# One block of a shared expert's tokens moved behind the routed experts in a one-core RWKV and mixture-of-experts layer

## The chip, the cores and the metric

The kernel runs on one core of a Trainium2 chip. The metric is the device time of one execution in microseconds (us). The median of three runs of the kernel before is 1152.21 us (1152.03 to 1153.88).

## What is computed

The input is x, 2048 tokens of 512 numbers in float32. Two parts follow each other. The first (time mixing and channel mixing) gives a new x. The second is a mixture of experts on h, the normalised x:

```python
x = x + attn(layernorm(x), ...)
h = layernorm(x)
scores = sigmoid(h @ gate_w)                      # 32 experts
sfc = scores + e_bias                             # chooses 2 of 4 groups, then 4 experts
combine = share of each chosen expert, 2.5 * score / sum of the 4 scores
routed = sum over the 4 experts of combine * relu(h @ Wu[e])**2 @ Wd[e]     # 512 -> 256 -> 512
shared = relu(h @ Wsu)**2 @ Wsd                                             # 512 -> 1024 -> 512
out = x + routed + shared
```

## The kernel before, in words

The program is written out engine by engine with semaphores. Nothing is scheduled by a planner: the order on each engine is the order of the code. Products in float32 precision are made of three matmuls of "hi" and "lo" halves (`split_product`, L595). A block is 512 tokens (`BLK`), a tile 128 (`P`). The shared expert's inner width of 1024 is cut into `NSI` = 8 slices of 128.

**Stages 1 and 2** compute the first part and are not touched.

**Stage 3** is the shared expert, in `NB` = 4 blocks of tokens (`pe_block3`, L1083). For each slice i, TensorE does `up(i)` (12 matmuls of 512 columns into bank 4 or 5) and then `down(i - 2)` (12 matmuls into banks 0 to 3, which sum over all slices). Between them ScalarE takes the bank through relu, squares it and makes the hi half (`act_inner`, L835), and GpSimd makes the lo half `ksp_lo` (`pool_inner`, L894). At a block's end ScalarE copies the four banks to `so` and SyncE's queue stores them to `shx_d`, the table in HBM on which half of the routed results are added later. The block's tokens come from HBM into the two slots of `hTb` (`sp_hTb`, L1216).

Beside stage 3, VectorE works out the routing (`routing_vector`, L1290): which tokens go to which expert, and from that a list of tiles, each of up to 128 tokens of one expert. It needs TensorE three times: `pe_counts` (L1108) and two calls of `pe_ids` (L1115). These stand in the blocks 1, 2 and 3, each behind slice 2 (`BETWEEN_AT`). When `rows_i` is there, GpSimd can begin to gather tokens (`first_gathers`, L1663), which it does behind its last `ksp_lo` of stage 3.

**Stage 4** is the routed experts: 84 tiles here. For each, GpSimd gathers 128 rows by an indirect DMA, TensorE transposes them (L1497), multiplies with `Wu` of the expert (L1505), transposes the result (L1513) and multiplies with `Wd` (L600). ScalarE scales the result into a ring of four buffers `yo` (`take_y`, L1575), and GpSimd adds it to rows in HBM by an indirect DMA with addition (`add_rows`, L1674): even tiles to `res_d` (which holds x), odd tiles to `shx_d`. Additions to one table must wait for each other. Weights of eight experts lie in a ring `w8`, loaded by SyncE's queue (`load`, L1222).

**Stage 5** waits until all additions have landed, loads `res_d` and `shx_d` in 8 parts each (`stage5_sync`), adds them on VectorE (`stage5_vector`) and stores the sums to `out` from ScalarE's queue (`stage5_scalar`).

```python
            pe_block3(pe, 0, router=True)
            pe_block3(pe, 1, between=pe_counts)
            pe_block3(pe, 2, between=lambda pe: pe_ids(pe, (0, 1)))
            pe_block3(pe, 3, between=lambda pe: pe_ids(pe, (2, 3)))
```

Of the kernel before, what the change touches and what calls it, by code (L numbers as in the profile page):

```python
# [24 lines left out]
P = 128  # L25
T, H = 2048, 512
NT = T // P
BT = 4
# [45 lines left out]
def program(nc, a, out, scratch):  # L74
# [13 lines left out]
    with ctx:  # L88
# [9 lines left out]
        shx_rows = shx_d[0:T].rearrange("(b j p) d -> b p j d", j=BT, p=P)  # L98
        spare_rows = [m[T:T + 2 * P].rearrange("(n p) (u d) -> p n u d", p=P, u=2) for m in (res_d, shx_d)]
# [69 lines left out]
        wsu = [at(f"wsu_{s}", [P, C, SI], R, 16 * n) for n, s in enumerate(("hi", "lo"))]  # L169
        wsd = [at(f"wsd_{s}", [P, NSI, H], R, 32 + 16 * n) for n, s in enumerate(("hi", "lo"))]  # L170
# [14 lines left out]
        ebias = at("ebias", [P, E], F, 182.0625)  # L185
# [15 lines left out]
        xg = [at(f"xg{n}", [P, H + E], F, 2.125 * (n % 6) + (186 if n < 6 else 64)) for n in range(XRING)]  # L201
# [8 lines left out]
        last = [at(f"last{n}", [P, 8, NT // 8 * H], F, kb) for n, kb in enumerate((104, 64))]  # L210
# [624 lines left out]
        def act_inner(act, n, i, router=None):  # L835
# [3 lines left out]
            nc.scalar.activation(ra[:, i % 2], bank[4 + i % 2][:], ACT.Relu).then_inc(sem("kc_free"), 1)  # L839
# [65 lines left out]
        def pe_inner_up(pe, n, i, weights, rhs):  # L905

            pe.wait_ge(sem("kc_free"), n + 1)
            split_product(bank[4 + i % 2][:], lambda s, c: weights[s][:, c, i * P:(i + 1) * P],
                          rhs, C).then_inc(sem("kc_in"), 1)

        def pe_inner_down(pe, n, i, last, rhs):

            pe.wait_ge(sem("klo_in"), n + 3)
            for j in range(BT):
                for k, (l, r) in enumerate(((0, 0), (0, 1), (1, 0))):
                    m = nc.tensor.matmul(bank[j][:], ksp[l][:, i % 2, j * P:(j + 1) * P], rhs(r),  # L916
                                         start=i == 0 and k == 0, stop=i == last and k == 2)
            m.then_inc(sem("vc_done"), 1)
# [162 lines left out]
        BETWEEN_AT = 2  # L1081

        def pe_block3(pe, b, router=False, between=None):  # L1083
# [17 lines left out]
            for i in range(NSI):  # L1101
                pe_inner(pe, NB - 1, i, N3 + b * NSI + i, up, down, router, NB * BT)
                if i == BETWEEN_AT and between:
                    between(pe)
# [65 lines left out]
        def stage3_scalar(act):  # L1170
            act_hi3(act, *ORDER3[:4])
            act_block3(act, 0, router=True)
            with act.Fori(1, NB) as b:
# [27 lines left out]
        def stage3_gpsimd(pool):  # L1201
            pool_block3(pool, 0, first=True)
            with pool.Fori(1, NB - 1) as b:
                pool_block3(pool, b)
            pool_block3(pool, NB - 1, last=True)
# [47 lines left out]
        def stage3_sync(sp):  # L1253

            sp.wait_ge(sem("trT_in"), NB * C)
# [12 lines left out]
            sp.wait_ge(sem("sc_in"), NB)  # L1268
            sp.dma_start(ebias[:], a["L0_ffn_e_bias"].partition_broadcast(P)).then_inc(sem("eb_in"), 16)
            for b in range(NB):  # L1270
                if b + 2 < NB:
                    sp.wait_ge(sem("kc_in"), N3 + (b + 1) * NSI)
                    sp.wait_ge(sem("hb_in"), 16 * (b + 2))
                    if b + 2 == NB - 1:
                        sp.wait_ge(sem("ht_st"), 16 * C * NB + 16)
                    sp_hTb(sp, b + 2)
                if b == 1:
                    first_experts(sp)
                if b == 1:
                    sp.wait_ge(sem("share_in"), 1)  # L1280
                    sp.wait_ge(sem("h_st"), 16 * NB + 16)
                    sp.dma_start(share_rows, share[:]).then_inc(sem("share_st"), 16)
                if b == 2:
# [536 lines left out]
```

## Time and profile before

| what | value |
|---|---|
| median of three runs | 1152.21 us |
| the profiled execution | 1152.85 us |
| its span | 1151.0 us |
| mean granted TensorE clock | 0.972 of 2.4 GHz |
| TensorE busy | 1058.1 us (92%) |
| VectorE, ScalarE, GpSimd busy | 574.8, 539.7, 436.0 us |
| DMA | 192.91 MB, mean 168 GB/s |

The span is the stretch from the first to the last instruction or transfer of the profiled execution; 1.85 us of its own time lie outside it. Shares are averages over stages with different limits, so each stage has to be read by itself.

### The profile page before, as it was taken

Reading aid. Unit: us, or ns where it says so; the run is one execution under the profiler, and the core shown is the slowest. Engines: PE = TensorE matmul, PEld = TensorE weight load, DVE = VectorE, ACT = ScalarE, POOL = GpSimd, SP = SyncE. Lnnn points to the kernel's source line nnn. Section 1 sums busy time; section 2 is a strip of 40 time slices with the busy share of each in tenths; the row PEclk is TensorE's granted clock in tenths of the full one; section 3 lists DMA queues with packets and bytes.
Section 4 is the critical chain, followed back from the end, with each engine's and each line's share of the span. In section 5 each row is a group of like instructions: output and inputs, shape, how many; then the busy total and the mean of one; then the engine's idle time right before and its main releaser. Section 6 shows DMA issues by size and latency. Waiting matters only on the chain.

```text
span 1151.0 us, 17191 instructions
## 1 busy us (share of the span) xinstructions
PE 1058.1 (92%) x4892; PEld 849.6 (74%) x4893; DVE 574.8 (50%) x1126; ACT 539.7 (47%) x896; POOL 436.0 (38%) x327
## 2 busy tenths in 40 slices
PE   1999989999999999999989999998999999999940
PEld 0446768888788878878867888886888888888830
DVE  6976764925570475320072886322545544455532
ACT  3643536333333333243353334335777766677730
POOL 1012212321222132112252234226767777888730
PEclk9898999999999999999998999998999999999985
DMA  8605176526421642342472228016898999988679
GB/s 285 228 1 183 55 249 249 179 74 219 147 92 60 233 158 97 121 150 95 131 289 110 110 111 265 37 37 162 168 282 182 247 233 270 327 140 136 84 137 373
DMA packets 96914, 192.91 MB, mean 168 GB/s; under 512 B 12888, under 2 KB 32344, under 8 KB 96352
## 3 DMA queue, kind: packets, MB, share of 16 engines
q1 hardware_dynamic: 76464, 147.43, 36.8%
q0 software_dynamic: 18816, 39.87, 18.5%
q10 hardware_dynamic: 1584, 4.98, 1.2%
q8 instruction: 27, 0.44, 0.1%
q14 instruction: 23, 0.19, 0.1%
HBM read 137.78 MB, written 60.03 MB: 172 GB/s over the span
## 4 chain that ended last, share of the span: by engine, by line
PE 82%; DMA 7%; DVE 7%; issue 2%; ACT 2%; SPq 1%; POOL 0%; ACTq 0%; POOLq 0%; DVEq 0%
PE bank L600 36%; PE bank L916 22%; PE bank L1505 11%; PE bank L517 4%; PE bank L1497 3%; DMA shx_d<-yo,idy 2%; DMA last<-shx_d 2%; PE bank L1513 1%; DMA res_d<-yo,idy 1%; PE bank L924 1%; SPq L1751 1%; PE bank L934 1%; DMA f<-in_L_attn_x 1%; DMA z_d<-zo 1%; PE bank L978 1%
## 5 line engine op out<-in xcount | busy, mean ns | idle before, releaser
L897 POOL TENSOR_TENSOR ksp_lo<-ra,ksp_hi 128x512 fp32r<-128x512 f32 x96 | 146.3, 1524 | 470.1 <-ACT ksp_hi L846 470.1
L1632 DVE TENSOR_TENSOR wds<-w,wds 128x1024 fp32r<-128x1024 f32 x84 | 103.1, 1227 | 186.4 <-ACT wds L1573 186.4
L1505 PE MATMUL bank<-w,xT 128*128 x672 | 160.3, 382 | 0.4 <-SPq L71 0.3
L916 PE MATMUL bank<-vring,ksp_hi 128*128 128x512 f32 x512 | 159.5, 393 | 0.0
L1505 PEld LDWEIGHTS bank<-w,xT 128*128 128x128 f32 x672 | 128.1, 191 | 21.1 <-issue 1.4
L839 ACT ACTIVATE ra<-bank 128x512 f32<-128x512 f32 x96 | 57.3, 597 | 173.9 <-PE bank L600 170.4
L600 PE MATMUL bank<-wds,aT 128*128 128x512 f32 x504 | 137.6, 408 | 1.4 <-DVE aT L1627 1.3
L846 ACT ACTIVATE ksp_hi<-ra 128x512 fp32r<-128x512 f32 x96 | 60.7, 632 | 124.9 <-PE bank L916 124.4
L916 PEld LDWEIGHTS bank<-vring,ksp_hi 128*128 128x128 f32 x512 | 95.6, 188 | 20.0
L600 PE MATMUL bank<-xcT_hi,wck_lo 128*128 128x512 f32 x256 | 101.8, 398 | 0.0
L600 PEld LDWEIGHTS bank<-wds,aT 128*128 128x128 f32 x504 | 88.5, 189 | 18.0 <-DVE aT L1627 1.8
L600 PE MATMUL bank<-xcT_lo,wck_hi 128*128 128x512 f32 x256 | 101.6, 397 | 0.0
L600 PE MATMUL bank<-xcT_hi,wck_hi 128*128 128x512 f32 x256 | 101.3, 396 | 0.0
L916 PE MATMUL bank<-vring,ksp_lo 128*128 128x512 f32 x256 | 99.9, 390 | 0.0
L1580 ACT ACTIVATE yo<-bank,xg 128x512 f32<-128x512 f32 x84 | 57.8, 688 | 85.7 <-PE bank L600 54.2
L1659 POOL DMA_INDIRECT xg<-h_d,idc x60 | 84.7, 1412 | 18.3 <-issue 16.2
L1573 ACT ACTIVATE wds<-w 128x1024 fp32r x84 | 88.1, 1049 | 0.1
L600 PE MATMUL bank<-hTb,wsu_hi 128*128 128x512 f32 x256 | 79.8, 393 | 0.0
L361 POOL TENSOR_TENSOR mix_lo<-mx,mix_hi 128x512 fp32r<-128x512 f32 x16 | 22.4, 1416 | 121.5 <-ACT mix_hi L419 121.5
L1681 POOL DMA_INDIRECT res_d<-yo,idy x36 | 58.0, 1612 | 26.3 <-DMA res_d<-yo,idy 13.5
L1681 POOL DMA_INDIRECT shx_d<-yo,idy x36 | 57.4, 1594 | 20.0 <-DMA shx_d<-yo,idy 9.3
L841 ACT ACTIVATE ra<-ra 128x512 f32<-128x512 f32 x96 | 60.7, 632 | 3.1
(260 smaller groups left out, 1916.4 us busy)
## 6 DMA issues: line engine op xcount, KB each, us to landing
vring<-wcv_d SPq DMA_DIRECT2D x64, 512.0 KB, 3.3
w<-in_L_ffn_Wu SPq DMA_DIRECT2D x32, 512.0 KB
w<-in_L_ffn_Wd SPq DMA_DIRECT2D x32, 512.0 KB
hT_d<-hT SPq DMA_DIRECT2D x16, 512.0 KB, 3.3
hTb<-hT_d SPq DMA_DIRECT2D x4, 2048.0 KB, 9.4
raw_wcv<-in_L_attn_Wcv SPq DMA_DIRECT2D x4, 1024.0 KB, 6.6
raw_wck<-in_L_attn_Wck SPq DMA_DIRECT2D x4, 1024.0 KB, 9.6
f<-in_L_attn_x SPq DMA_DIRECT2D x4, 1024.0 KB, 6.9
```

Of the source, the lines that this page charges most:

```text
L600: i = nc.tensor.matmul(dst, lhs(l, c), rhs(r, c), start=c == 0 and k == 0, stop=c == n - 1 and k == 2)
L839: nc.scalar.activation(ra[:, i % 2], bank[4 + i % 2][:], ACT.Relu).then_inc(sem("kc_free"), 1)
L841: nc.scalar.activation(ra[:, i % 2], ra[:, i % 2], ACT.Square).then_inc(sem("sq"), 1)
L846: nc.scalar.activation(ksp[0][:, i % 2], ra[:, i % 2], ACT.Copy).then_inc(sem("khi_in"), 1)
L897: nc.gpsimd.tensor_tensor(ksp[1][:, i % 2], ra[:, i % 2], ksp[0][:, i % 2], ALU.subtract).then_inc(sem("klo_in"), 1)
L916: m = nc.tensor.matmul(bank[j][:], ksp[l][:, i % 2, j * P:(j + 1) * P], rhs(r), start=i == 0 and k == 0, stop=i == last and k == 2)
L1505: m = nc.tensor.matmul(bank[2 + u][:, 0:EI], xT4[:, u, c * P:(c + 1) * P], slot_of(wu8[:, :, c * EI:(c + 1) * EI], e), start=c == 0, stop= ...
L1573: nc.scalar.activation(wds[:, u, 0], slot_of(wd8, e), ACT.Copy).then_inc(sem("wh4"), 1)
L1580: nc.scalar.activation(yo[:, t % YRING], bank[6 + u][:], ACT.Copy, scale=xg[t % XRING][:, bass.ds(H + e, 1)]).then_inc(sem("y4"), 1)
L1632: nc.vector.tensor_tensor(wds[:, u, 1], slot_of(wd8, e), wds[:, u, 0], ALU.subtract).then_inc(sem("wl4"), 1)
L1659: pool.indirect_dma_start(out=xg[t % XRING][:], out_offset=None, in_=h_d, in_offset=bass.IndirectOffsetOnAxis(ap=row.bitcast(U32), axis=0) ...
L1681: pool.indirect_dma_start(out=(res_d, shx_d)[u], out_offset=bass.IndirectOffsetOnAxis(ap=row.bitcast(U32), axis=0), in_=yo[:, k % YRING], ...
```

## The change

One block of the shared expert, tokens 1536 to 2047, leaves stage 3 and is computed behind the last routed tile. TensorE does `up3(0)` and `up3(1)` between its last three steps of stage 4, then the other slices (banks 0 and 1 for up, 2 to 5 for down). ScalarE and GpSimd do their part of it behind their last `take_y` and `add_rows`. `hT3`, the block's tokens, is loaded into two slots of the weight ring when expert 25 is done. The rows of `shx_d` of this block no longer hold the shared expert's result: they are set to zero by eight stores before, and in stage 5 VectorE adds the block's sums straight out of the four banks. Stage 5 now has six parts of 256 rows for the other 1536 tokens and a part `rest` for these 512. It loads all of `res_d` as soon as that table's additions have landed, then `shx_d`, and all stores go out from SyncE's queue.

The routing's TensorE work stands earlier: `pe_counts` behind slice 1 of block 1, `pe_ids` behind slices 1 and 4 of block 2. The bias `ebias` is loaded at the start of stage 3 instead of behind the scores. The buffers of stage 4 (`xT4`, `a4`, `aT4`, `yo`, `wds`, half of `xg`) lie elsewhere, because the weights of the shared expert must stay in place. Weight loads of experts 0 to 6 are issued in block 1 and not in blocks 1 and 2.

```diff
+        hT3 = at("hT3", [P, 2, C, BLK], R, 96)
...
-        xT4 = at("xT4", [P, 2, C * P], F, 0)
-        a4 = at("a4", [P, 2, EI], F, 8)
-        aT4 = at("aT4", [P, 2, 2, EI], R, 10)
-        yo = at("yo", [P, YRING, H], F, 14)
-        wds = at("wds", [P, 2, 2, EI // P * H], R, 34)
+        xT4 = at("xT4", [P, 2, C * P], F, 160.5)
+        a4 = at("a4", [P, 2, EI], F, 92.75)
+        aT4 = at("aT4", [P, 2, 2, EI], R, 180.5)
+        yo = at("yo", [P, YRING, H], F, 172.5)
+        wds = at("wds", [P, 2, 2, EI // P * H], R, 64)
...
-        last = [at(f"last{n}", [P, 8, NT // 8 * H], F, kb) for n, kb in enumerate((104, 64))]
+        PARTS = 6
+        last = [at(f"last{n}", [P, PARTS, 2 * H], F, kb) for n, kb in enumerate((112, 136))]
+        rest = [at(f"rest{n}", [P, BT, H], F, kb) for n, kb in enumerate((64, 72))]
...
-            pe_block3(pe, 1, between=pe_counts)
-            pe_block3(pe, 2, between=lambda pe: pe_ids(pe, (0, 1)))
-            pe_block3(pe, 3, between=lambda pe: pe_ids(pe, (2, 3)))
+            pe_block3(pe, 1, between={1: pe_counts})
+            pe_block3(pe, 2, between={1: lambda pe: pe_ids(pe, (0, 1)), 4: lambda pe: pe_ids(pe, (2, 3))})
...
+            for n in range(BT):
+                for u in range(2):
+                    sp.dma_start(open_rows[:, n, u], zrow[:].bitcast(F)).then_inc(sem("spare_st"), 16)
...
             dve.wait_ge(sem("eb_in"), 16)
-            dve.wait_ge(sem("num_in"), 2)
+            dve.wait_ge(sem("sc_in"), NB)
+            dve.wait_ge(sem("ht_st"), 16 * C * NB + 16)
...
+        def up3(pe, i):
+            pe_inner_up(pe, N4 + i, i, wsu, lambda s, c: hT3[:, s, c], kc=0)
+
+        def down3(pe, i):
+            pe_inner_down(pe, N4 + i, i, NSI - 1, lambda s: wsd[s][:, i], to=2)
...
             final = GROUP * passes + GROUP - 1
+            pe.wait_ge(sem("hb_in"), 16 * NB)
             turn(final, 1)
+            up3(pe, 0)
             down(final - 1, 0)
+            up3(pe, 1)
             down(final, 1)
+            for i in range(2, NSI):
+                up3(pe, i)
+                down3(pe, i - 2)
+            down3(pe, NSI - 2)
+            down3(pe, NSI - 1)
...
+            end = sp.value_load(ends_i[0:1, E - WSLOTS + 1:E - WSLOTS + 2], min_val=1, max_val=SLOT_TILES)
+            wait_apart(sp, sem("d4"), end + 2)
+            sp.dma_start(hT3[:].bitcast(F), hT_d[NB - 1]).then_inc(sem("hb_in"), 16)
...
-            for u in range(2):
+            for u, rows in enumerate((res_d, shx_d)):
                 wait_apart(sp, sem(f"y_st{u}"), 8 * GROUP * passes + 8 * GROUP)
+                for n in range(PARTS):
+                    sp.dma_start(last[u][:, n], part_rows(rows)[:, n]).then_inc(sem(f"part_in{n}"), 16)
+                sp.dma_start(rest[u][:], rest_rows(rows)).then_inc(sem(f"part_in{PARTS}"), 16)
             for n in range(PARTS):
-                for to, rows in zip(last, (res_d, shx_d)):
-                    sp.dma_start(to[:, n], part_rows(rows[0:T])[:, n]).then_inc(sem(f"part_in{n}"), 16)
+                sp.wait_ge(sem("o5"), n + 1)
+                sp.dma_start(part_rows(out[0])[:, n], last[0][:, n]).then_inc(sem("o_st"), 16)
+            for j in range(BT):
+                sp.wait_ge(sem("o5"), PARTS + 1 + j + 1)
+                sp.dma_start(rest_rows(out[0])[:, j], rest[0][:, j]).then_inc(sem("o_st"), 16)
+            sp.wait_ge(sem("o_st"), 16 * (PARTS + BT))
...
+            dve.wait_ge(sem(f"part_in{PARTS}"), 16 + 32)
+            nc.vector.tensor_tensor(rest[0][:], rest[0][:], rest[1][:], ALU.add).then_inc(sem("o5"), 1)
+            dve.wait_ge(sem("o5"), PARTS + 1)
+            for j in range(BT):
+                dve.wait_ge(sem("sum3"), j + 1)
+                nc.vector.tensor_tensor(rest[0][:, j], rest[0][:, j], bank[2 + j][:], ALU.add).then_inc(sem("o5"), 1)
...
         def stage5_scalar(act):
-            for n in range(PARTS):
-                act.wait_ge(sem("o5"), n + 1)
-                act.dma_start(part_rows(out[0])[:, n], last[0][:, n]).then_inc(sem("o_st"), 16)
-            act.wait_ge(sem("o_st"), 16 * PARTS)
+            for i in range(NSI):
+                act_inner(act, N4 + i, i, kc=0)
+
+        def stage5_gpsimd(pool):
+            for i in range(NSI):
+                pool_inner(pool, N4 + i, i)
```

Two places show how the order of instructions moves. The first is TensorE at the end of stage 4. `ident,a` is the transpose of a tile's inner values, `wds,aT` the product with `Wd` of six matmuls a tile. Before, these are its last instructions (x12 are the last two tiles):

```order
L1513 MATMUL bank<-ident,a_195 128x128 x2
L600 MATMUL bank<-wds,aT_196 128x512 x6
L1513 MATMUL bank<-ident,a_195 128x128 x2
L600 MATMUL bank<-wds,aT_196 128x512 x12
L88 UNCONDITIONAL_BRANCH
```

In the change, from the same transpose on (`hT_149` is the tile `hT3`):

```order
L1522 MATMUL bank<-ident,a_196 128x128 x2
L604 MATMUL bank<-wds,aT_197 128x512 x6
L1522 MATMUL bank<-ident,a_196 128x128 x2
L604 MATMUL bank<-hT_149,wsu_hi 128x512 x2
L604 MATMUL bank<-hT_149,wsu_lo 128x512
L604 MATMUL bank<-hT_149,wsu_hi 128x512 x2
L604 MATMUL bank<-hT_149,wsu_lo 128x512
L604 MATMUL bank<-hT_149,wsu_hi 128x512 x2
L604 MATMUL bank<-hT_149,wsu_lo 128x512
L604 MATMUL bank<-hT_149,wsu_hi 128x512 x2
L604 MATMUL bank<-hT_149,wsu_lo 128x512
L604 MATMUL bank<-wds,aT_197 128x512 x6
```

Twelve matmuls of `up3(0)` now stand ahead of the product of the last tile but one, and another twelve (`up3(1)`) ahead of that of the last tile; the remaining 168 follow.

The second place is SyncE's queue at the end of the program. Before, from the last weight load on, it holds the reads of `passes_i` and 16 loads in turns; two pairs of the eight are shown:

```order
L1226 DMA w_181<-in_L_ffn_Wd 128x2x512
L1730 REGISTER_ALU
L1730 COMPARE_AND_BRANCH
L1460 TENSOR_LOAD passes_i
L1460 ISA x2
L70 ISA
L1751 DMA last_201<-res_d 128x1024
L1751 DMA last_202<-shx_d 128x1024
L1751 DMA last_201<-res_d 128x1024
L1751 DMA last_202<-shx_d 128x1024
L1751 DMA last_201<-res_d 128x1024
L1751 DMA last_202<-shx_d 128x1024
```

In the change:

```order
L1759 DMA hT_149<-hT_d 128x4096
L1463 TENSOR_LOAD passes_i
L1463 ISA x2
L70 ISA
L1771 DMA last_202<-res_d 128x1024 x6
L1772 DMA rest_204<-res_d 128x4x512
L1771 DMA last_203<-shx_d 128x1024 x6
L1772 DMA rest_205<-shx_d 128x4x512
L1775 DMA out<-last_202 128x1024 x6
L1778 DMA out<-rest_204 128x512 x4
L88 UNCONDITIONAL_BRANCH
```

The load of `hT3` is new, the two tables are no longer loaded in turns, and the stores of the result have moved to this queue.

## Rows read from the trace of the kernel before

**Rows 1.** The page: the chain that ended last, by engine; costly groups.

```profile
PE 82%; DMA 7%; DVE 7%; issue 2%; ACT 2%; SPq 1%; POOL 0%; ACTq 0%; POOLq 0%; DVEq 0%
...
L1505 PE MATMUL bank<-w,xT 128*128 x672 | 160.3, 382 | 0.4 <-SPq L71 0.3
...
L839 ACT ACTIVATE ra<-bank 128x512 f32<-128x512 f32 x96 | 57.3, 597 | 173.9 <-PE bank L600 170.4
L600 PE MATMUL bank<-wds,aT 128*128 128x512 f32 x504 | 137.6, 408 | 1.4 <-DVE aT L1627 1.3
```

**Rows 2.** Chain of waits, 700 to 800 us: start, length (us), what.

```profile
700.12 1.38 PE bank L1121 x32
...
734.25 8.16 PE bank L600 x36
...
745.13 1.38 PE bank L1121 x32
...
749.34 2.72 PE bank L916 x12
...
771.10 8.17 PE bank L916 x36
...
784.05 1.94 PE bank L1497 x8
...
786.07 3.31 PE bank L1505 x8
```

**Rows 3.** Timeline of GpSimd, 700 to 790 us: start, length, instruction, [idle before].

```profile
774.62 1.29 POOL L897 TENSOR_TENSOR ksp_lo<-ra,ksp_hi 128x512 fp32r<-128x512 f32 x1 [4.15 <-ACT ksp_hi L846]
776.09 1.22 POOL L1659 DMA_INDIRECT xg<-h_d,rows_i  x1 [0.18 <-issue]
```

**Rows 4.** Timeline of TensorE, 1095 us to the end.

```profile
1104.60 0.44 PE L1513 MATMUL bank<-ident,a 128*128 128x128 f32 x2 [0.59 <-DVE a L1623]
1104.93 1.64 PE L600 MATMUL bank<-wds,aT 128*128 128x512 f32 x6
1107.92 1.66 PE L600 MATMUL bank<-wds,aT 128*128 128x512 f32 x6 [1.34 <-DVE aT L1627]
```

**Rows 5.** Timeline of ScalarE, then of GpSimd, 1084 to 1112 us.

```profile
1109.73 0.69 ACT L1580 ACTIVATE yo<-bank,xg 128x512 f32<-128x512 f32 x1 [2.24 <-DMA shx_d<-yo,idy]
...
1111.40 1.54 POOL L1681 DMA_INDIRECT shx_d<-yo,idy  x1 [1.48 <-DMA shx_d<-yo,idy]
```

**Rows 6.** Chain of waits, the last 51 us.

```profile
1100.67 1.73 PE bank L1505 x8
...
1111.40 4.51 DMA shx_d<-yo,idy
...
1115.98 0.35 SPq L1751
...
1124.77 21.91 DMA last<-shx_d
...
1146.70 1.23 DVE last L1756
```

**Rows 7.** Busy time by stretch: PE, PEld, DVE, ACT, POOL, then PEclk, DMA share, GB/s.

```profile
784.00:788.00 4.00, 3.87 (x13) 3.15 (x14) 0.05 (x1) 2.14 (x3) 3.09 (x4) 0.50 1.03 368
1108.00:1112.00 4.00, 1.58 (x6) 0.97 (x6) 0.00 (x0) 0.69 (x1) 2.14 (x2) 1.00 0.83 100
1121.00:1126.00 5.00, 0.00 (x0) 0.00 (x0) 2.45 (x2) 0.00 (x0) 0.00 (x0) 0.50 1.02 370
1136.00:1146.00 10.00, 0.00 (x0) 0.00 (x0) 3.22 (x3) 0.00 (x0) 0.00 (x0) 0.50 1.02 419
```

**Rows 8.** Timeline of VectorE, 612 us to the end.

```profile
673.14 2.29 DVE L1405 TENSOR_TENSOR hot_p<-iota_p,small 128x2048 f16<-128x2048 f32 x1
...
700.93 2.29 DVE L1405 TENSOR_TENSOR hot_p<-iota_p,small 128x2048 f16<-128x2048 f32 x1 [13.21 <-PE bank L1121]
...
712.90 1.76 DVE L1410 TENSOR_TENSOR hot_q<-hot_f,token 128x1536 f16<-128x1536 f16 x1
...
728.32 0.15 DVE L1434 TENSOR_SCALAR passes_i<-passes_i 128x1 int32<-128x1 int32 x1
...
1121.01 1.22 DVE L1756 TENSOR_TENSOR last<-last,last 128x1024 f32<-128x1024 f32 x1 [13.15 <-DMA last<-shx_d]
```

**Rows 9.** Timeline of GpSimd, 600 to 701 us: one slow `ksp_lo`.

```profile
673.64 2.94 POOL L897 TENSOR_TENSOR ksp_lo<-ra,ksp_hi 128x512 fp32r<-128x512 f32 x1 [4.14 <-ACT ksp_hi L846]
```

More of the change, by code:

```diff
@@ L98, in program @@
         shx_rows = shx_d[0:T].rearrange("(b j p) d -> b p j d", j=BT, p=P)
+        open_rows = shx_d[T - BLK:T].rearrange("(n p) (u d) -> p n u d", p=P, u=2)
         spare_rows = [m[T:T + 2 * P].rearrange("(n p) (u d) -> p n u d", p=P, u=2) for m in (res_d, shx_d)]
@@ L184, in program @@
         top8 = at("top8", [P, NT, 8], F, 181.5625)
-        ebias = at("ebias", [P, E], F, 182.0625)
+        ebias = at("ebias", [P, E], F, 200)
         small = at("small", [P, 8, NT * GROUPS], F, 182.1875)
@@ L903, in stage2_gpsimd, with pe_inner_up, pe_inner_down @@
                     pool_inner(pool, b * NCI + i, i)
-        def pe_inner_up(pe, n, i, weights, rhs):
+        def pe_inner_up(pe, n, i, weights, rhs, kc=4):
             pe.wait_ge(sem("kc_free"), n + 1)
-            split_product(bank[4 + i % 2][:], lambda s, c: weights[s][:, c, i * P:(i + 1) * P],
+            split_product(bank[kc + i % 2][:], lambda s, c: weights[s][:, c, i * P:(i + 1) * P],
                           rhs, C).then_inc(sem("kc_in"), 1)
-        def pe_inner_down(pe, n, i, last, rhs):
+        def pe_inner_down(pe, n, i, last, rhs, to=0):
             pe.wait_ge(sem("klo_in"), n + 3)
@@ L915, in pe_inner_down @@
                 for k, (l, r) in enumerate(((0, 0), (0, 1), (1, 0))):
-                    m = nc.tensor.matmul(bank[j][:], ksp[l][:, i % 2, j * P:(j + 1) * P], rhs(r),
+                    m = nc.tensor.matmul(bank[to + j][:], ksp[l][:, i % 2, j * P:(j + 1) * P], rhs(r),
                                          start=i == 0 and k == 0, stop=i == last and k == 2)
-            m.then_inc(sem("vc_done"), 1)
+                if to and i == last:
+                    m.then_inc(sem("sum3"), 1)
+            if not (to and i == last):
+                m.then_inc(sem("vc_done"), 1)
         def pe_logits(pe, b, c):
@@ L1102, in pe_block3 @@
                 pe_inner(pe, NB - 1, i, N3 + b * NSI + i, up, down, router, NB * BT)
-                if i == BETWEEN_AT and between:
-                    between(pe)
+                if i in between:
+                    between[i](pe)
             down(NSI - 2)
@@ L1172, in stage3_scalar @@
             act_block3(act, 0, router=True)
-            with act.Fori(1, NB) as b:
+            with act.Fori(1, NB - 1) as b:
                 act_block3(act, b)
@@ L1202, in stage3_gpsimd @@
             pool_block3(pool, 0, first=True)
-            with pool.Fori(1, NB - 1) as b:
-                pool_block3(pool, b)
-            pool_block3(pool, NB - 1, last=True)
+            pool_block3(pool, 1)
+            pool_block3(pool, NB - 2, last=True)
         def sp_raw3(sp, k):
@@ L1253, in stage3_sync @@
         def stage3_sync(sp):
+            sp.dma_start(ebias[:], a["L0_ffn_e_bias"].partition_broadcast(P)).then_inc(sem("eb_in"), 16)
             sp.wait_ge(sem("trT_in"), NB * C)
@@ L1267, in stage3_sync @@
             sp_hT(sp, NB - 1)
[L1268 to L1276, printed above, removed]
+            for n in range(BT):
+                for u in range(2):
+                    sp.dma_start(open_rows[:, n, u], zrow[:].bitcast(F)).then_inc(sem("spare_st"), 16)
+            for b in range(NB - 1):
+                if b == 0:
+                    sp.wait_ge(sem("kc_in"), N3 + NSI)
+                    sp.wait_ge(sem("hb_in"), 16 * 2)
+                    sp_hTb(sp, 2)
                 if b == 1:
                     first_experts(sp)
-                if b == 1:
                     sp.wait_ge(sem("share_in"), 1)
@@ L1604, in stage4_scalar @@
             a_hi(0, 0)
+            act.wait_ge(sem("bs_st"), 16 * NB)
             for t in range(2, YRING + 2):
@@ L1777, in _ @@
             stage4_gpsimd(pool)
+            stage5_gpsimd(pool)
         @block.scalar
```

27 lines of the change are left out of this document (13 added, 14 removed).

## The prediction

> **What bounds the kernel now.** I read the page's chain first, then the chain in order of time around the block that moves, the timelines of the engines where stage 3 ends and where stage 4 ends, and busy time by stretch. TensorE is 82% of the chain, and in stage 4 its two large groups of matmuls waited 0.4 and 1.4 us in all [rows 1]. So whatever leaves TensorE's queue before the last tile comes off the time in full. The block that moves is one unbroken run of TensorE work, from 734.25 to 779.27 us, 45.0 us, of which `pe_ids` has 1.4 to 1.5 [rows 2]. The reader should then look at the other end. TensorE starts its last product at 1107.92 [rows 4], and from there the program is one chain: ScalarE's last scaling at 1109.73 and GpSimd's last addition at 1111.40 [rows 5], its landing at 1115.91, the loads of both tables until 1146.68, one VectorE addition until 1147.93, and the store, with which the span ends at 1151.0 [rows 6]. In those 41.4 us TensorE has nothing to do. The change puts 43.5 us of it there, so the question is by how much the new TensorE work sticks out behind the transfers.
>
> **What leaves stage 3.** 192 matmuls, at 2.72 us for 12 [rows 2]: 43.5 us. The `pe_ids` of block 3 goes to block 2 and keeps its 1.4. What follows stage 3 hangs on its last block and moves with it: the first gather was issued 0.18 us after the last `ksp_lo` [rows 3], and TensorE stood still from 779.27 to 784.05 before its first transposes [rows 2]. I keep this gap as it was. Its cover is the routing: in block 2 everything must be known 43.5 us sooner. VectorE stood still 13.21 us because `pe_ids` had its place behind slice 2 of block 2 [rows 8]. Behind slice 1 it starts one up and one down earlier, 5.44 us, and VectorE's next masks with it: the fourth pair, done at 714.66, would be done near 709.2. TensorE reaches its new place for it, behind slice 4, at about 712.5 (slice 3 begins at 701.5, when the first `pe_ids` is done [rows 2]; four runs of 2.72, the 1.4 of `pe_ids` in them before and after alike). That leaves some 3 us. The list of owners (728.47) comes at 723.0 and the list of rows about 1.5 us later, ahead of the last `ksp_lo` of block 2, now near 731. Nothing waits, so the routing's part of the change is worth nothing by itself. Of `ebias` the same holds.
>
> **The other edits of stage 3.** The eight zero stores of 128 KB and the earlier weight loads stand on SyncE's queue behind the stores of `hT` and in block 1, where the next load of tokens is wanted tens of us later; cost nothing. If that cover were gone, TensorE would start block 2 late. The load of `hT3` (2 MB) goes out when expert 25 is done and is wanted only behind the last tile. It competes with gathers and additions, as 1 MB of weights for each expert did all through stage 4, where TensorE lost under 2 us in all [rows 1]; nothing, at most 2 us. The moved buffers have the same sizes and readers; nothing.
>
> **What is added behind stage 4**, in the times of the trace of before, so that the 43.5 us are taken off at the end. The turn of the last tile starts at 1104.60 and what follows it at 1104.93 [rows 4].
> - `up3(0)` 2.72, product of the last tile but one 1.36 (half of 12), `up3(1)` 2.72: the last product starts at 1111.73, 3.8 us later than before.
> - ScalarE began its scaling 1.81 us after that product's start [rows 4, 5]: 1113.54 to 1114.23.
> - Only then comes its first relu, 0.60 [rows 1], which frees a bank. `up3(2)` starts at 1114.95 and ends at 1117.67. TensorE has stood still from 1113.1, 1.8 us.
> - `down3(0)` wants `ksp_lo`, on GpSimd behind the last addition. That was issued 0.98 us after the scaling and took 1.54 [rows 5]: 1115.21 to 1116.75. `ksp_lo` takes 1.29 [rows 3], to 1118.04. 0.4 us of waiting.
> - Eight downs and five ups, 13 times 2.72: 35.4 us, to 1153.5.
> - VectorE's last addition out of a bank has half the columns of the 1.23 us one [rows 6]; I take 0.7, with 0.25 to wake. Then the store until the end of the span, 3.07 [rows 6]: 1157.5.
>
> **Sum.** 1157.5 less 43.5 is a span of 1114.0, against 1151.0: 37.0 us less. The profiled execution's own time was 1152.85, which gives 1115.8; it lies 0.64 above the median, so from the median I forecast **1115.2 us**.
>
> **The cover of the loads.** Loads and stores must be done before TensorE, or they are the bound. Before, from the first issue (1115.98) to the last landing (1146.68) [rows 6], 16 loads and some 7 stores of 0.524 MB moved, 12.1 MB in 30.7 us. Now `res_d` can start when its last addition has landed: the product starts at 1107.65, and with the 1.81, 0.69, 0.98 and 4.5 us above [rows 5, 6] that is 1115.6. The other table's addition lands near 1120, hidden behind 4.2 MB of loads. So 8.4 MB of loads and 6 stores, 11.5 MB, at the same pace take 29.3 us, to 1145.3. VectorE's addition of the 2048 columns of `rest` is twice 1.23, to 1147.8. TensorE's first bank is ready nine matmuls before its end, at 1151.4. There are 3.6 us to spare. At the 370 GB/s of the first stretch of loads [rows 7] it would be 1.9 us more, at 419 it would be sooner. The page *DMA: Bandwidth & Descriptors* of the Trainium skill (section Bandwidth, "Where 436 GB/s comes from") puts what HBM gives a core at about 358 GB/s; by that, an estimate, the 11.5 MB take 32.2 us, with 2.2 us until the stream runs (the first MB was there after 5.0 us [rows 6, 8]) `rest` would be added only at 1152.6, and the sum would be about 1 us more. The trace speaks against it, since 10 us of mixed loads and stores ran at 419 GB/s.
>
> **The rivals.**
> - *The DMAs are the bound.* Place: `rest`, last of 14 loads, behind six stores. For it: the share of the DMA engines is 1.02 in both stretches [rows 7], so nothing hides there, and the last addition to `shx_d` now has to land beside 4 MB of loads. If the loads of `shx_d` start only at 1130, 4.2 MB and 3.1 MB of stores take 18.6 to 19.8 us, and the additions of `rest` and of four banks end near 1155: about 1116. With a slower pace yet, up to 1121. Against: 3.6 us to spare. Chance 0.14.
> - *GpSimd's last `ksp_lo` waits for VectorE.* One `ksp_lo` took 2.94 us where 1.29 is usual, while VectorE was in the 2.29 us mask that began half a microsecond before it [rows 3, 8, 9]. The page *GPSIMD Engine Reference* of the Trainium skill (section Key points) says the two share their SBUF interfaces, when VectorE has two SBUF inputs; the trace agrees. The last `ksp_lo` falls near 1148.8, just where `rest` (2.45 us, two inputs) may be added. TensorE wants it 0.65 us after its usual end, so the loss is up to 1.8 us: 1115.2 to 1117.0. The other seven have some 6 us to spare. Chance 0.16.
> - *The routing is late.* If VectorE gains nothing by the earlier `pe_ids` (its fourth pair at 714.66 as now), TensorE waits 2.2 us at slice 4: 1117.4. More if the gathers wait too. Chance 0.06.
> - *Slower: TensorE runs the tail at its lower clock.* Place: the stops of 0.6, 1.8 and 0.4 us at the seam. After the stop of 4.8 us the granted clock was 0.50 (1.2 GHz), and 8 matmuls took 3.31 us [rows 2, 7] where stage 4's usual step has the same for 1.73 [rows 6]; so the price is 0.91 us for each us of matmuls. Over all 46 us of the tail that is 42 us, and the time 1157. It decides from 41 us of the tail at the lower clock on. Against: after the stop of 1.34 us the last six took 1.66, like the six before (1.64) [rows 4], and the clock was 1.00 in that stretch [rows 7]. A single spell like that at 784 would cost 2 to 4 us. Chance 0.03 for slower.
> - *The work is not taken off the front*, or stage 4 pays for it: something in block 2 or among the first tiles waits for what block 3 used to cover (the eighth expert's weights, gathers beside a busy VectorE), by 7 us to 35 us: 1122 to 1150. I see nothing for it in the rows. Chance 0.05.
>
> **How the numbers follow.** The forecast as it stands has 0.56. Its own range is 1113.5 to 1117: below because the last store is now 256 KB instead of 512, above for `hT3`. To that the first three rivals are added, all below 1121; what is left out is the last two and a little on either side. Range 1113.0 to 1121.0. A measurement of this kernel can tell 0.2%, 2.3 us, from no change. All cases but the slower one and the far end of the last are faster by more: 0.96 faster, 0.01 within, 0.03 slower.
>
> **What would show it.** Right: stage 4's first transposes near 740.5; TensorE's block at the end unbroken for 13 runs of 2.72 us, with one stop of about 1.8 us before `up3(2)` and one under 1 us before `down3(0)`; its last matmul 3.5 to 4.5 us before the end of the span; VectorE adds `rest` before it waits for a bank; and the chain, read from its end, goes to TensorE and not to the loads. Wrong: an addition of `rest` that ends after TensorE (DMA bound), a `ksp_lo` above 2 us as the last one, a stop at L1126 (`pe_ids`) in block 2, a granted clock of 0.50 behind the seam, or first transposes later than 742.

## The result, and the profile after

The changed kernel took 1123.3 us (median of four runs), the kernel before 1152.12 us beside it: a ratio of 0.973, interval 0.970 to 0.977. The forecast was 1115.2 us with a range of 1113.0 to 1121.0. So the sign and most of the gain came as forecast, and some 8 us of it did not. One of the four runs, of 1206.88 us at a granted clock of 0.856 where the others had 0.984 to 0.989, is left out of the ratio, and the median of the other three is 1122.99 us. The profiled execution took 1123.62 us, 1.92 us more than its span.

The page: span, busy time of each engine, shares of its chain, and the second of the two groups of matmuls of [rows 1]:

```profile
span 1121.7 us, 17152 instructions
...
PE 1061.7 (95%) x4892; PEld 849.4 (76%) x4893; DVE 580.5 (52%) x1129; ACT 536.4 (48%) x892; POOL 434.3 (39%) x327
...
PE 74%; DMA 7%; DVE 7%; issue 6%; POOL 3%; ACT 2%; POOLq 0%; DVEq 0%; ACTq 0%; SPq 0%
...
L604 PE MATMUL bank<-wds,aT 128*128 128x512 f32 x504 | 138.2, 410 | 1.4 <-DVE aT L1645 1.3
```

The chain of the changed kernel where stage 3 ends, in order of time (start, length, what), which answers to [rows 2]:

```profile
728.51 8.17 PE bank L920 x36
...
737.89 3.56 issue
741.45 1.91 PE bank L1506 x8
```

Stage 3 now ends at 736.69 and the first transposes start at 741.45, after the same gap of 4.76 us. Forecast was 740.5. The front of the program is as forecast, but for 0.9 us.

The chain of the tail, which answers to [rows 6], and the timeline of VectorE in it (start, length, engine, line, operation, in brackets the idle time before and what ended it):

```profile
1069.96 8.22 PE bank L604 x36
...
1078.32 0.70 ACT yo L1597
...
1079.81 1.54 POOL shx_d L1699
1081.35 1.33 POOL ksp_lo L901
...
1082.72 3.02 PE bank L920 x12
...
1110.22 6.13 PE bank L920 x27
...
1116.45 2.66 DVE rest L1790 x4
```

```profile
1096.42 9.09 DVE L1784 TENSOR_TENSOR last<-last,last 128x1024 f32<-128x1024 f32 x6 [23.25 <-DMA last<-shx_d]
1105.49 2.29 DVE L1786 TENSOR_TENSOR rest<-rest,rest 128x2048 f32<-128x2048 f32 x1
1116.45 2.66 DVE L1790 TENSOR_TENSOR rest<-rest,bank 128x512 f32<-128x512 f32 x4 [8.67 <-PE bank L920]
```

The program now ends with TensorE, not with the loads: VectorE has added `rest` and stands still 8.67 us until TensorE's first bank is there. The last tile's turn is at 1069.55, and from it to the end of the span are 52.15 us. The forecast had 52.9 (1104.60 to 1157.5).

So the stretch in which the time went astray is the one that the change seemed to leave alone, stage 4:

| stretch | before | forecast | after | after less forecast |
|---|---|---|---|---|
| start to first transposes | 784.05 | 740.5 | 741.45 | +0.9 |
| first transposes to last tile's turn | 320.55 | 320.55 | 328.10 | +7.55 |
| last tile's turn to end of span | 46.40 | 52.9 | 52.15 | -0.7 |
| span | 1151.0 | 1114.0 | 1121.7 | +7.7 |

A tile of stage 4 takes TensorE 3.775 us where nothing is waited for. I took the starts of all 84 tiles' `Wu` products from the timeline; what the distance from one to the next has above 3.775 is called the tile's loss. Tiles are counted from 0. Before, five tiles between 928 and 1002 us lost 0.3 to 1.0 us each, 3.0 together. After, eight between 868 and 962 us lost 0.4 to 1.3 each, 5.0 together, and three others stand out: the third tile (tile 2, 749 us) with 1.67, and tiles 70 and 71 (1012 and 1020 us) with 3.81 and 0.77. These last two are the largest piece, 4.58 us. There the trace has, on SyncE's queue, GpSimd, ScalarE and TensorE:

```profile
1001.15 0.35 SPq L1759 DMA_DIRECT2D hT<-hT_d  x1
1001.91 1.58 POOL L1699 DMA_INDIRECT res_d<-yo,idy  x1 [0.31 <-issue]
...
1014.25 1.58 POOL L1699 DMA_INDIRECT res_d<-yo,idy  x1 [4.98 <-DMA res_d<-yo,idy]
...
1013.59 0.69 ACT L1597 ACTIVATE yo<-bank,xg 128x512 f32<-128x512 f32 x1 [5.68 <-DMA res_d<-yo,idy]
...
1013.94 0.60 PE L1506 MATMUL bank<-ident,xg 128*128 128x128 f32 x4
1017.14 0.44 PE L1522 MATMUL bank<-ident,a 128*128 128x128 f32 x2 [2.59 <-DVE a L1641]
1017.47 2.54 PE L604 MATMUL bank<-wds,aT 128*128 128x512 f32 x6
```

and in the chain, which runs through it:

```profile
1001.91 11.55 DMA res_d<-yo,idy
```

The load of `hT3` is issued at 1001.15, an addition to `res_d` right behind it at 1001.91, and that addition lands only after 11.55 us. Before, the last addition took 4.5 us [rows 6], and four in the middle of its stage 4, beside weight loads, took 7.3 to 9.1. ScalarE may not overwrite its `yo`, so it stands still 5.68 us and takes no bank, VectorE gets nothing, and TensorE stands still 2.59 us. Then its six matmuls take 2.54 us instead of the usual 1.38 to 1.40. The windows (us; PE, PEld, DVE, ACT, POOL busy, granted clock, share of the DMA engines, GB/s) show why:

```profile
1004.00:1008.00 4.00, 4.00 (x23) 3.43 (x22) 2.14 (x4) 2.91 (x6) 3.53 (x5) 1.00 1.04 398
1008.00:1012.00 4.00, 4.00 (x23) 3.44 (x22) 1.02 (x3) 0.00 (x0) 1.27 (x1) 1.00 0.96 262
1012.00:1016.00 4.00, 2.54 (x14) 2.00 (x12) 0.48 (x1) 2.42 (x5) 1.58 (x1) 1.00 0.36 98
1016.00:1020.00 4.00, 2.86 (x9) 2.20 (x10) 3.27 (x6) 2.81 (x6) 3.26 (x3) 0.75 0.83 132
1020.00:1024.00 4.00, 4.00 (x20) 3.37 (x19) 1.73 (x4) 2.89 (x5) 3.39 (x3) 0.83 0.95 150
```

First the DMA engines are full (1.04, 398 GB/s), then ScalarE does nothing for 4 us, then TensorE has a hole, and after the hole the granted clock is 0.75 and 0.83: part of these 8 us ran at 1.2 GHz and not at 2.4.

The kernel before has the first half of this pattern on a smaller scale. There the two weight loads of one expert, 0.5 MB each, stand right ahead of an addition (SyncE's queue, then the chain, then GpSimd):

```profile
917.10 0.38 SPq L1224 DMA_DIRECT2D w<-in_L_ffn_Wu  x1
917.58 0.46 SPq L1226 DMA_DIRECT2D w<-in_L_ffn_Wd  x1
...
917.64 9.12 DMA res_d<-yo,idy
...
927.57 1.58 POOL L1681 DMA_INDIRECT res_d<-yo,idy  x1 [2.55 <-DMA res_d<-yo,idy]
```

The addition lands after 9.12 us, and the tile at 928 us, the first of the five above, loses 0.77. In both traces the small losses lie during such series of weight loads or up to 11 us behind one. No run takes the weight loads away, so that these cause the small losses is not shown.

The tile at 749 us, and one in stage 3 where a half product waited for GpSimd:

```profile
752.81 1.62 PE L604 MATMUL bank<-wds,aT 128*128 128x512 f32 x6 [1.35 <-DVE aT L1645]
687.18 0.47 PE L920 MATMUL bank<-wsd_hi,ksp_hi 128*128 128x512 f32 x1 [0.28 <-POOL ksp_lo L901]
```

### The profile page after: what moved, and what is told of

It is laid out like the page before. It is cut to its first block, busy times and chain, and to the rows that moved or that the text cites. A ratio compares the mean times of both kernels' runs of the same rounds, so it can differ in the third digit from the quotient of the medians.

```text
span 1121.7 us, 17152 instructions
## 1 busy us (share of the span) xinstructions
PE 1061.7 (95%) x4892; PEld 849.4 (76%) x4893; DVE 580.5 (52%) x1129; ACT 536.4 (48%) x892; POOL 434.3 (39%) x327
## 4 chain that ended last, share of the span: by engine, by line
PE 74%; DMA 7%; DVE 7%; issue 6%; POOL 3%; ACT 2%; POOLq 0%; DVEq 0%; ACTq 0%; SPq 0%
PE bank L604 34%; PE bank L920 22%; PE bank L1514 7%; PE bank L521 5%; DMA res_d<-yo,idy 4%; DMA shx_d<-yo,idy 2%; PE bank L1506 2%; PE bank L931 1%; PE bank L1522 1%; POOL shx_d L1699 1%; POOL xg L1677 1%; PE bank L941 1%; DMA f<-in_L_attn_x 1%; PE bank L985 1%; DVE bns L311 1%
## 5 line engine op out<-in xcount | busy, mean ns | idle before, releaser
L1677 POOL DMA_INDIRECT xg<-h_d,idc x60 | 81.1, 1351 | 18.3 <-issue 16.5
L604 PE MATMUL bank<-hTb,wsu_hi 128*128 128x512 f32 x192 | 60.1, 394 | 1.1 <-DMA hTb<-hT_d 1.1
```

What stands on the lines that cost most here:

```text
L604: i = nc.tensor.matmul(dst, lhs(l, c), rhs(r, c), start=c == 0 and k == 0, stop=c == n - 1 and k == 2)
L1677: pool.indirect_dma_start(out=xg[t % XRING][:], out_offset=None, in_=h_d, in_offset=bass.IndirectOffsetOnAxis(ap=row.bitcast(U32), axis=0) ...
```

## The experiments

All are edits of the changed kernel. The theory: the load of `hT3`, one DMA of 2 MB with 16 KB for each partition, gets in the way of an addition, and that costs the 4.6 us. Rivals: the place itself (short tiles there), the wait for `bs_st` at 749 us, or nothing but scatter. The first four ran beside a kernel before of 1154.22 us.

**The changed kernel again**, no edit.

> The changed kernel once more, unedited, to see how much of the 7.7 us that it lies above the forecast is the same in every execution. In its first trace the routed tiles lost 8.6 us against a steady 3.775 us for each tile; 1.7 of that behind the first three tiles, 3.8 and 0.8 right behind the load of hT3, and the rest in steps of 0.3 to 1.3 us between 867 and 966 us. Theory A (two fixed costs of the change, the wait for the store of the shared expert and the load of hT3): the first and the hT3 losses come again at the same tiles within 0.5 us, the others wander; span 1118 to 1123. Theory B (chance of the DMAs only): the losses lie elsewhere, and the span is anywhere from 1114 to 1124.

Measured: 1118.57 us (1115.74 to 1123.6), ratio 0.9695 (0.965 to 0.974). The profiled execution, 1120.71 us, has the loss at the same two tiles, 3.11 and 1.04, with an addition that landed after 11.09 us. The stop at the third tile is not in it. So theory A holds for the load and fails for the third tile; and the kernel scatters by 8 us.

**The load left out.**

```diff
-            pe_inner_up(pe, N4 + i, i, wsu, lambda s, c: hT3[:, s, c], kc=0)
+            pe_inner_up(pe, N4 + i, i, wsu, lambda s, c: wsd[s][:, c], kc=0)
...
-            pe.wait_ge(sem("hb_in"), 16 * NB)
...
-            end = sp.value_load(ends_i[0:1, E - WSLOTS + 1:E - WSLOTS + 2], min_val=1, max_val=SLOT_TILES)
-            wait_apart(sp, sem("d4"), end + 2)
-            sp.dma_start(hT3[:].bitcast(F), hT_d[NB - 1]).then_inc(sem("hb_in"), 16)
```

> The load of hT3 (2 MB) and the wait for it are left out; the moved block then multiplies by wsd where it should by hT3, with the same shapes, so its result is another. Theory A: the load keeps additions waiting, one landing took 11.6 us, and cost 4.6 us at two tiles; time 4 to 5 us below the unedited kernel, and no tile period above 5 us after 1000 us. Theory B: the additions are at their limit anyway and the loss only moves; under 2 us below the unedited kernel.

Measured: 1115.49 us (1110.48 to 1118.42), ratio 0.9656 (0.961 to 0.970). The stretch in its windows, whole where the kernel with the load has its hole:

```profile
1008.00:1012.00 4.00, 4.00 (x23) 3.45 (x22) 1.90 (x3) 3.10 (x7) 3.08 (x4) 1.00 0.85 142
1012.00:1016.00 4.00, 4.00 (x23) 3.45 (x22) 1.90 (x3) 2.94 (x6) 3.39 (x3) 1.00 0.87 149
1016.00:1020.00 4.00, 4.00 (x23) 3.45 (x22) 1.90 (x3) 3.02 (x6) 3.39 (x3) 1.00 0.80 140
```

No tile after 966 us lost anything. The load is the cause of that loss, not the place. By the medians it is worth 3.1 us here (1118.57 less 1115.49), where 4 to 5 were expected, and the two ranges overlap.

**The wait for `bs_st` moved** to the first tile's `take_y`, the first writer of a `yo`.

```diff
+                elif t == 0:
+                    act.wait_ge(sem("bs_st"), 16 * NB)
...
-            act.wait_ge(sem("bs_st"), 16 * NB)
```

> ScalarE waits for the store of so to shx_d only right before it writes yo for the first tile, not ahead of the relu and copies of the tiles 1 to 4. Theory A: the store was issued at 738.9 and the wait ended at about 751.2, 2.5 us after ScalarE could have gone on; the first use of yo is at about 753, so the stop vanishes and TensorE's first product starts 1.3 to 1.7 us sooner; time 1.3 to 1.7 us less. Theory B: the store is not what ended that wait, or the time is lost again at the first additions, which are behind the same store; under 0.5 us.

Measured: 1118.84 us (1117.95 to 1123.76), ratio 0.971 (0.967 to 0.975), no different from the unedited kernel: theory B, or a stop that comes too seldom to show in a median. Tiles 70 and 71 lose 3.65 and 0.75.

**The same 2 MB in rows of 2 KB**, eight DMAs one behind the other.

```diff
-            sp.dma_start(hT3[:].bitcast(F), hT_d[NB - 1]).then_inc(sem("hb_in"), 16)
+            for s in range(2):
+                for c in range(C):
+                    sp.dma_start(hT3[:, s, c].bitcast(F), hT_d[NB - 1][:, s, c]).then_inc(sem("hb_in"), 16)
```

> The load of hT3 goes out at the same moment and with the same bytes, but as eight DMAs whose rows are 2 KB instead of one with rows of 16 KB. Theory A1 (the long rows keep the additions from their turn on each DMA engine): the loss behind 1001 us falls from 4.6 to under 2 us; time 3 to 4 us below the unedited kernel. Theory A2 (it is the bytes: 2 MB at once take 5 to 6 us of all engines whatever their rows): the loss stays 4 to 5 us.

Measured: 1116.36 us (1115.52 to 1117.6), ratio 0.9679 (0.965 to 0.971), 2.2 us below the unedited kernel. GpSimd's and TensorE's rows, which answer to those at 1014.25 and 1017.14 of the changed kernel, and a window:

```profile
1007.95 1.58 POOL L1699 DMA_INDIRECT res_d<-yo,idy  x1 [2.98 <-DMA res_d<-yo,idy]
1010.84 0.44 PE L1522 MATMUL bank<-ident,a 128*128 128x128 f32 x2 [0.60 <-DVE a L1641]
```

```profile
1012.00:1016.00 4.00, 4.00 (x23) 3.44 (x22) 2.22 (x4) 3.38 (x9) 3.39 (x3) 1.00 0.86 149
```

The same bytes from the same tile on: the addition lands after 9.55 us instead of 11.1 to 11.6, TensorE stops 0.60 us, the clock stays at 1.00, and the two tiles lose 0.98 us in place of 4.2 to 4.6. So 2 us less of landing took 3 us or more off the loss, since the last 2 us of delay also bring the lower clock. That is theory A1's outcome for the loss. But the edit changes two things. Each of the eight DMAs has its own issue on SyncE's queue, and the eight take 5.21 us (from 996.86) where the one of 2 MB took 0.35. Short rows and a load that goes out spread over 5 us can't be told apart by this run.

The next four ran beside a kernel before of 1153.19 us. **Two DMAs with rows of 8 KB:**

```diff
+            for s in range(2):
+                sp.dma_start(hT3[:, s].bitcast(F), hT_d[NB - 1][:, s]).then_inc(sem("hb_in"), 16)
```

> The load of hT3 at the same moment as two DMAs with rows of 8 KB, between the one with 16 KB (tiles 70 and 71 lost 3.8 and 0.8 us, or 3.1 and 1.0) and the eight with 2 KB (1.0 us in all). If the length of a row is what keeps an addition waiting, the loss lies between, 2 to 4 us, and the addition's landing between 9.6 and 11.6 us. If the number of DMAs matters and not the rows, it is nearer to 4.6 us.

Measured: 1118.96 us (1114.61 to 1125.88), ratio 0.9707 (0.967 to 0.975); landing 11.41 us, stop 2.45 us, loss 3.36 and 1.10. As 16 KB, and so the outcome that was expected if not the rows matter but the number of DMAs. The two are issued within 0.84 us. By this run the spread issue is at least as good an explanation of the eight DMAs' gain as their short rows; the rows of 16 KB sent as eight DMAs, over fewer partitions each, would tell more, and were not run.

**One piece a tile**, the eight pieces each behind a tile of their own:

```diff
+            for s in range(2):
+                for c in range(C):
+                    wait_apart(sp, sem("d4"), end + (2 + s * C + c))
+                    sp.dma_start(hT3[:, s, c].bitcast(F), hT_d[NB - 1][:, s, c]).then_inc(sem("hb_in"), 16)
```

> The same eight pieces with rows of 2 KB, but each waits for one tile more, so that 256 KB go out every 3.8 us instead of 2 MB at once. Theory A: what is left of the loss behind expert 25 (1.0 us) goes too, all tiles from 60 on take 3.775 us, and the time is 0 to 1 us under that of the small rows sent at once (1116.4 median). Rival: SyncE's waits cost something that I don't see, or pieces late in the stage meet the last additions; 1 us or more above it.

Measured: 1116.57 us (1115.73 to 1118.65), ratio 0.9674 (0.965 to 0.970). Nothing is lost after 966 us, as expected; the medians of this and of small rows alone are 0.2 us apart, less than they scatter.

**Small rows, and the seam closed:** ScalarE and GpSimd do slices 0 and 1 of the moved block ahead of the last two `take_y` and `add_rows`, not behind both.

```diff
+                    act_inner(act, N4 + k - n, k - n, kc=0)
                     take_y(passes, t - 2, t % 2, before)
...
+                    if last and k >= GROUP - 2:
+                        pool_inner(pool, N4 + k - GROUP + 2, k - GROUP + 2)
                     add_rows(i, k, idy[:, k:k + 1])
...
-            for i in range(NSI):
+            for i in range(2, NSI):
```

> The small rows at once, and in addition ScalarE takes the moved block's slices 0 and 1 through relu, square and hi half ahead of its last two scalings, and GpSimd their lo halves ahead of its last two additions. The stops of TensorE behind the last routed tile (1.4 us before up3(2), 0.2 and a slower first matmul before down3(0)) should vanish, the last additions come 0.3 to 1.5 us later, which nothing waits for, since rest was added 8.7 us before its first bank. Expected 1.4 to 1.7 us less than the small rows alone, 1114.8 in the median. Rival: the stops reappear elsewhere (TensorE's products of the last two tiles wait), 0 to 0.5 us less.

Measured: 1113.77 us (1112.68 to 1114.95), ratio 0.9652 (0.963 to 0.967). At the seam TensorE has no idle time behind the last turn any more (the last product of stage 4, then `up3(2)`, then `down3(0)`):

```profile
1069.17 1.52 PE L604 MATMUL bank<-wds,aT 128*128 128x512 f32 x6
1070.53 0.62 PE L604 MATMUL bank<-hT,wsu_hi 128*128 128x512 f32 x2
...
1073.25 0.39 PE L920 MATMUL bank<-wsd_hi,ksp_hi 128*128 128x512 f32 x1
```

From `up3(2)` to `down3(0)` are 2.72 us; in the changed kernel, with a slow start and the stop of 0.17, 1079.55 to 1082.72 are 3.17, and the stop of 1.37 stands ahead of it. The gain is more than the 1.4 to 1.7 us expected: 2.6 us in the medians (of two batches), and 2.2 in the traces from the last turn on.

**Pieces paced, and the seam closed**, the last two diffs together, the pieces one a tile:

> One piece of hT3 a tile, and the seam as in the run before: the two gains add, 1113.5 to 1115.5 us in the median, below both the kernel before and the changed one.

Measured: 1113.72 us (1112.21 to 1116.43), ratio 0.9659 (0.964 to 0.968). As expected. Either of the two beats both kernels, and they don't differ.

The last four were to put a number on the load, beside a kernel before of 1154.0 us. **A second load of `hT3`**, seven tiles behind the first:

```diff
             sp.dma_start(hT3[:].bitcast(F), hT_d[NB - 1]).then_inc(sem("hb_in"), 16)
+            sp.wait_ge(sem("hb_in"), 16 * NB)
+            wait_apart(sp, sem("d4"), end + 9)
+            sp.dma_start(hT3[:].bitcast(F), hT_d[NB - 1]).then_inc(sem("hb_in"), 16)
```

> The load of hT3 issued a second time, seven tiles after the first, with the same 2 MB and the same rows of 16 KB; the result is unchanged. If the load is what holds the addition back and stops TensorE: a second loss of 4 to 4.6 us appears some 27 us after the first (near 1040), with an addition to res_d or shx_d that lands after 11 us, and the time is 4 to 5 us above the unedited kernel of this batch. Rival, the loss at tiles 70 and 71 belongs to that place (short tiles of one expert, a low clock there) and not to the load: no second loss, and the time is that of the unedited kernel within 1 us.

**The unedited kernel, the kernel without the load, and the one with rows of 2 KB**, with the edits shown above:

> The changed kernel as it is, as the measure for the other three of this batch. Expected: a median between 1118 and 1122, with the loss of 4.2 to 4.6 us at tiles 70 and 71 in the trace.

> The load of hT3 and the wait for it left out again; the moved block's up products read the weights of wsd in its place, so that the shared expert's share of tokens 1536 to 2047 is something else. If the load's price is what its stretch of the trace shows, the median is 4 to 5 us below the unedited kernel of this batch, near 1115. Rival, the price is partly made good elsewhere or hidden by the scatter: 1 to 3 us.

> hT3 loaded by eight DMAs with rows of 2 KB at the same moment. By the traces so far it keeps 1.0 us of the loss: the median 3 to 4 us below the unedited kernel of this batch, near 1116, and about 1 us above the kernel without the load. If both differ by under 1 us from the unedited one, the loss that the trace shows is not what sets the time.

| kernel | median us (range) | ratio (interval) |
|---|---|---|
| loaded twice | 1118.82 (1118.41 to 1121.0) | 0.971 (0.969 to 0.973) |
| unedited | 1119.14 (1115.93 to 1124.99) | 0.970 (0.969 to 0.972) |
| no load | 1116.68 (1115.49 to 1118.13) | 0.968 (0.966 to 0.970) |
| rows of 2 KB | 1116.89 (1114.42 to 1117.06) | 0.968 (0.966 to 0.969) |

GpSimd's and TensorE's rows of the kernel with two loads, at the first and at the second, and a window behind the first stop:

```profile
1009.21 1.58 POOL L1699 DMA_INDIRECT res_d<-yo,idy  x1 [3.76 <-DMA res_d<-yo,idy]
1012.09 0.44 PE L1522 MATMUL bank<-ident,a 128*128 128x128 f32 x2 [1.37 <-DVE a L1641]
...
1025.47 0.35 SPq L1762 DMA_DIRECT2D hT<-hT_d  x1
1036.87 1.58 POOL L1699 DMA_INDIRECT shx_d<-yo,idy  x1 [3.33 <-DMA shx_d<-yo,idy]
1040.03 0.44 PE L1522 MATMUL bank<-ident,a 128*128 128x128 f32 x2 [1.17 <-DVE a L1641]
```

```profile
1012.00:1016.00 4.00, 3.91 (x20) 3.26 (x21) 2.27 (x5) 3.38 (x7) 3.26 (x3) 1.00 0.84 142
```

and the stop in the unedited kernel of the same batch:

```profile
1018.90 0.69 PE L1522 MATMUL bank<-ident,a 128*128 128x128 f32 x2 [2.80 <-DVE a L1641]
1019.24 2.92 PE L604 MATMUL bank<-wds,aT 128*128 128x512 f32 x6
```

The second load makes a second stop, at another tile and on the other table: the mechanism is the load's, wherever it is put. But my size for it missed. Each of the two costs 1.74 and 1.54 us here, since both stops were short and the clock stayed at 1.00; the one load of the unedited trace beside it costs 4.42, with a stop of 2.80 us and six matmuls that took 2.92. Up to the first stop the two programs are the same, so the size of the stop is a matter of the execution too. The loss has two parts: a stop of 1.2 to 2.8 us, and what TensorE is slower behind it. That second part is 0.4 us behind the short stops, and 1.6 to 2.0 us behind the long ones, where the clock fell.

The medians say less. The kernel with two loads is 0.3 us below the one with one, where 4 to 5 above was expected: the second load's 1.54 us of the trace can't be seen in them. The one load costs 2.5 us in this batch (1119.14 less 1116.68), where I had expected 4 to 5, and rows of 2 KB keep 0.2 of it. Over all batches the medians are 1119.49 in thirteen executions of the unedited kernel, 1116.68 in nine without the load and 1116.89 in nine with small rows: 2.8 us for the load. That it costs something is clear (95 of the 117 pairs of an execution with and one without have the one with the load longer), but its size is only known to lie between about 1 and 6 us (95% interval of the shift, by ranks). The executions whose traces I have of the unedited kernel took 1120.71 to 1124.99 us, the upper half of its thirteen, and so their 4.2 to 4.6 is the upper part of what the load costs.

## Why the prediction was right, and where it failed

- **What leaves stage 3: right.** The block's 43.5 us came out: the run before the gap ends at 736.69 instead of 779.27, 42.6 us earlier. Of the missing 0.9, 0.44 was there before stage 3 began (its first turn at 606.54 against 606.10; over the runs it lay between 605.1 and 609.4), and 0.46 was lost in block 1 where TensorE waited for a `ksp_lo` of some 2 us behind VectorE's masks, at 687.18. That is the mechanism of the rival on GpSimd, at a place where I had not looked. The gap of 4.8 stayed, and TensorE had no stop at either `pe_ids` (695.62 and 713.43, 1.38 us each). The routing was ready as worked out, and its rival is out.
- **The other edits: the load of `hT3` is the step that failed.** It was put at "nothing, at most 2 us", because 1 MB of weights for each expert had done no harm. It cost 4.6 us in the profiled execution and 2.8 us in medians. Three things were wrong. The weights had not been harmless: right behind a pair of them an addition took 9.12 us, and five tiles lost 3.0 us between them, where the "under 2 us" of [rows 1] counts only TensorE's idle time ahead of two groups of matmuls. The load is twice what stood ahead of an addition before, one DMA of 2 MB against two of 0.5 MB issued 0.5 us apart. And I priced only the transfer, not what follows a stop: [rows 7] showed a stop of 4.8 us with the clock at 0.50 behind it, and I used that row for the seam alone. The rival "stage 4 pays for it" had 0.05 and a price of 7 to 35 us, so the right kind of case stood there, at the wrong size and without this cause.
- **The rest of stage 4: right, but for one execution.** 1.67 us at the third tile, where ScalarE now waits for `bs_st`, was in one trace of the changed kernel and in no other; moving the wait bought nothing. In that trace the first tile was shorter, and the start of stage 4 up to the fourth tile took 12.82 us against 11.84 before, 1.0 us more. The small losses between 868 and 962 us were 2.0 us larger than their like before. Such losses are in every trace, of before too; I did not test what sets them. With the load paced, the stretch from the first transposes to the last turn is 320.45 and 320.63 us in the two traces, against the 320.55 that the forecast took over from before. So without the load's harm the forecast for stage 4 holds.
- **Behind stage 4: right within 0.7 us.** Forecast were stops of 1.8 and 0.4 us; they were 1.37 and 0.17. ScalarE's first relu took 0.59, `ksp_lo` began behind the last addition, and then TensorE ran its 13 slices unbroken, one of 3.02 and twelve of 2.72 us. What was given away at the seam can be had: with the order changed the median is 1113.77 against 1116.36 with small rows alone, and from the last turn to TensorE's last matmul the two traces have 46.71 and 48.88 us.
- **The cover of the loads: right, and larger.** 3.6 us to spare were forecast, 8.7 measured. The DMA rival is out; `rest` was added at 1105.49 and TensorE's bank was wanted at 1116.45. The estimate by the 358 GB/s of the page *DMA: Bandwidth & Descriptors* (section Bandwidth) of the Trainium skill would have had `rest` about a microsecond too late; the trace speaks against it here too, with 415 GB/s of loads from 1088 to 1092 us.
- **GpSimd's last `ksp_lo`: out.** The row at 1113.75 has 1.29 us, VectorE being done with `rest` by then.
- **The lower clock in the tail: out.** The granted clock was 1.00 from 1076 to 1088, and only the twelve matmuls of `down3(0)` took 3.02 in place of 2.72. The mechanism was real, but in the middle of stage 4.
- **The sum.** 0.9 + 7.55 - 0.7 makes the 7.7 us between the span of 1121.7 and the forecast 1114.0. But the 1123.3 us are themselves from the long end of the scatter: the median of the thirteen executions is 1119.49, 4.3 us above the forecast and inside its range, so 3.8 of the 8.1 us are which executions were measured first. Of the 4.3, the load is 2.8. Without the load the kernel takes 1116.7, 1.5 us above the forecast and in its own range of 1113.5 to 1117; what the 1.5 are is open.

What stays open: why executions of one program lie up to 9 us apart (the longer ones have a granted clock of 0.984 to 0.987, the shorter ones 0.988 to 0.992, and the program reaches stage 3 up to 4 us earlier or later), and whether eight DMAs do little harm by their short rows or because they go out over 5 us. The two DMAs with rows of 8 KB, which do as much harm as the one, speak rather for the second.

## What to carry to other kernels

A large load that is wanted late is not free because its queue is idle and its bytes are few: look at which small transfers share the DMA engines in its first 12 us, how deep the ring behind them is, and pace it in small pieces, so that none of them lands later than that ring covers. Price a stall of TensorE together with the slow stretch that may follow it, and before you call similar loads harmless, look at how late the small transfers right behind them landed. And where a trace and a median disagree, look first at which execution was traced.

## What the runs showed of the hardware

- One DMA of 2 MB made an indirect addition of 128 rows, issued 0.8 us behind it, land after 11.1 to 11.8 us in four traces. In a fifth it was some 10.3 (an estimate: issued at 998.08, ScalarE went on at 1008.54), with the second of two loads 9.6, with eight DMAs of 2 KB rows 9.2 to 9.6, and with one piece for each tile no tile was late. Behind the two weight loads of an expert it was 9.12 in the kernel before, and up to 9.75 in the other traces, so the small rows bring it down to what weights do. The page *DMA: Bandwidth & Descriptors* of the Trainium skill (section Queues, rings and completion order) says that each engine changes between its queues at the end of a packet, and by that larger descriptors ahead of the addition's mean a longer turn. The traces count one packet a row: with one, two and eight DMAs they have 144, 289 and 1152 packets more than without the load, for 128, 256 and 1024 rows and 16 for each DMA. The small rows agree with the page, but they also went out over 5 us; the rows of 8 KB, with 11.41 us, do not bear it out.
- Stops of 2.13 us (the changed kernel again), 2.41, 2.45, 2.59 and 2.80 were each followed by one or two windows of 4 us with a granted clock of 0.57 to 0.91; those of 0.20 to 1.37 us there, or behind the second load, by none. In the 4 us windows ahead of the stop TensorE had been busy throughout, at 2.4 GHz.
- A `ksp_lo` on GpSimd takes 1.29 us alone and 1.5 to 3.4 us beside VectorE's masks, and one of 2.05 us made TensorE wait 0.28 us at 687.18, where the order leaves it no slack.
